# An audio tower on one core: the code is masked where it lies in PSUM, a ring of three banks, and small matmuls on halves of the array

## The chip, the cores and the metric

The kernel runs on one core of a Trainium2 chip. A core has TensorE (matmuls, results go to PSUM banks), ScalarE, VectorE, GpSimd (which works in SBUF) and DMA queues started here by SyncE. The metric is the device time of one execution in microseconds (us), the median of several runs.

## The reference

The input is `x` (16 items of 750 rows by 64). Each item goes through two layers. Layer 0: a recurrent token mixer with a strided 15-tap convolution (750 rows become S = 375), a retention with rotary embedding, and a product-key memory. Layer 1: a gradient step on a small two-layer model, then an expert layer for each item. Nearly all of the time is the product-key memory. Cut to what matters, it is, for each of 8 heads:

```python
sim = einsum('pbnhd,pkhd->pbnhk', q, pk_keys)          # p = 2 halves, 64 keys each
scores, idx = top_k(sim, 16)
score = scores[0][..., :, None] + scores[1][..., None, :]  # 256 candidates
final_scores, pk_idx = top_k(score, 16)
weights = softmax(final_scores)                         # on 16 of 4096 slots
# the 16 slots' keys and values are summed with these weights, then attended to
```

A row's 16 final slots, out of 64 x 64 = 4096, get softmax weights. Keys and values of the table (4096 x 8 heads, 64 + 64 columns) are summed with these weights for each of the 375 rows. An attention over the 375 sums per head and an output projection follow.

## The kernel before

One item has 375 rows, which stand in the free dimension (or as 3 tiles of 125 rows). VectorE finds for each row the 16 best keys of either half (`pick_rows`, the search) and turns them into three *factors* per head: `ranksT` (for each key of one half its rank, and how far the other half may reach), `first_of` (the exponential of the first half's score, fp32) and `second_of` (that of the second half, in bf16 pieces, two factors). The 16 x 4096 choice is never gathered. Instead the kernel rebuilds the dense weights of 128 table slots at a time. That is a *step*. There are 32 steps a head, 256 an item (`STEPS`), 4096 in all, and each goes through three engines in a software pipeline (`dense_slot`):

1. TensorE, the code (L527): `hot` x `ranksT` gives a value that is at most 0 where the slot was chosen and positive where it was not, in the bank `coded`.
2. ScalarE, the mask (L910): relu of the code, written as bf16 to `past` in SBUF.
3. TensorE, the spread (L506): the second half's values, spread over the 128 slots, and behind it in the same bank L508, which subtracts 1024 x `past` by a matmul with the diagonal `far`.
4. ScalarE (L905): relu of that bank to `dense_w` in SBUF. What was masked becomes 0. `taken` counts this.
5. GpSimd (L451, `weigh`): `dense_w` times `first_of`, in place.
6. TensorE (L520): table x `dense_w`, fp32, two instructions, summed over the head's 32 steps in `accu`.

A *slot* j of the pipeline holds on TensorE, in this order: the spread of step j-2, a factor if one is due, the sum of step j-6, the code of step j. On ScalarE it holds: `dense_w` of step j-2, the copy of a factor if one is due, the mask of step j. Each engine takes its own instructions strictly in that written order, and semaphores join them. `bank_free` makes TensorE wait until the bank that it is about to write was read. Before, the spreads and factors took turns in two banks (item n waits for item n-2), and `coded` was a third bank of its own, so that the code of step j waits for the mask of step j-1.

Factors of head 0 are made ahead of slot 0. Those of the other heads come in every second slot, in slots 0 to 6 and 30 to 76, one each, 28 in all: `ranksT` and the two `second_of` in bf16, `first_of` in fp32.

The rest of an item's work is written between slots, by constants (`FILL_PREPARE`, `STEPS_A`, ...). `prepare` is the token mixer, convolution and retention of item b+2 (33 slots in between). `gradient` is layer 1 of item b (30 slots). Then come 108 slots beside the search, with `similarities` (L608) in three places. `attention` holds the other 91 slots: per head the scores (L638), the query projection of head h+2 (L631), 5 slots, `mix` of head h-1 (L644), the transposes (L684), and 5 slots more. ScalarE's exponentials (L977) stand between its two groups of slots. After the last item a short tail runs the expert layer.

In this tower a matmul of 64 rows runs on a row half of the array, one of 64 output columns on a column half.

## Time and profile before

| | |
|---|---|
| median of 3 runs | 6943.39 us (6937.87 to 6958.16) |
| the profiled execution's own time | 6937.05 us |
| its span | 6935.2 us |
| TensorE busy | 6277.6 us, 91% of the span |
| ScalarE busy | 4668.2 us, 67% |
| GpSimd busy | 4397.3 us, 63% |
| VectorE busy | 4120.9 us, 59% |
| chain that ended last | TensorE 71%, GpSimd 12%, ScalarE 10%, VectorE 6% |
| mean granted TensorE clock | 0.983 of full speed |

A matmul's time in the trace runs from its start to the landing of its last column, so matmuls that follow each other overlap in the records. What a matmul costs TensorE is the distance from its start to the next one's start. In the same way ScalarE's instructions overlap: what one costs is the distance between starts. An item takes about 400 us in the steady part (the stretch from 3000 to 3400 us is one, and rows below are from it).

### The profile page before, as it was taken

How to read it: one execution, taken by the hardware profiler on the slowest of the kernel's cores; microseconds unless marked ns; L12 is line 12 of the kernel's file. 1: busy time of each engine (PE TensorE's matmuls, PEld its weight loads, DVE VectorE, ACT ScalarE, POOL GpSimd, SP SyncE). 2: the span in 40 equal slices, each digit the busy share in tenths (PEclk: the TensorE clock that was granted, in tenths of full speed). 3: DMA queues.
4: the chain of work that ended last, by engine and by line, in shares of the span. 5: the costliest groups of instructions: out<-in, count | busy, mean ns of one | idle time of the engine just before them, and what ended most of it. 6: DMA issues, size and time to landing. Idle time of an engine off the chain costs nothing.

```text
span 6935.2 us, 87978 instructions
## 1 busy us (share of the span) xinstructions
PE 6277.6 (91%) x28800; PEld 3567.8 (51%) x28800; DVE 4120.9 (59%) x13328; ACT 4668.2 (67%) x10873; POOL 4397.3 (63%) x4108
## 2 busy tenths in 40 slices
PE   2799999999999999999999999999999999999977
PEld 1455555555555555555555555555555555555533
DVE  7564847647484764748575574757557475752147
ACT  0676777767677776767676777767777776767733
POOL 0575857758585775858576585857668585766600
PEclk9999999999999999999999999999999999999978
DMA  1111111111111111111111111111111111111100
GB/s 33 43 49 38 46 42 43 48 37 48 38 49 39 45 47 37 49 36 49 39 46 45 37 49 36 52 36 46 46 36 49 38 51 37 46 47 43 44 19 15
DMA packets 93493, 290.94 MB, mean 42 GB/s; under 512 B 17879, under 2 KB 26546, under 8 KB 92780
## 3 DMA queue, kind: packets, MB, share of 16 engines
q1 hardware_dynamic: 92748, 285.25, 12.4%
q8 instruction: 229, 3.75, 0.2%
q14 instruction: 228, 1.87, 0.1%
q10 hardware_dynamic: 288, 0.07, 0.0%
HBM read 280.68 MB, written 4.61 MB: 41 GB/s over the span
## 4 chain that ended last, share of the span: by engine, by line
PE 71%; POOL 12%; ACT 10%; DVE 6%; issue 2%; DMA 0%; SPq 0%; DVEq 0%; ACTq 0%
PE accu L520 29%; POOL dense_w L451 12%; PE dense L527 8%; PE dense L506 7%; PE dense L508 7%; PE sims L638 3%; PE work L644 2%; ACT past L910 2%; PE work L631 1%; PE work L566 1%; PE sims L608 1%; PE work L684 1%; PE dense L492 1%; ACT dense_w L905 1%; PE work L618 1%
## 5 line engine op out<-in xcount | busy, mean ns | idle before, releaser
L451 POOL TENSOR_TENSOR dense_w<-dense_w,store 128x375 f32<-128x375 f32 x4096 | 4394.9, 1088 | 2208.8 <-ACT dense_w L905 2126.5
L520 PE MATMUL accu<-dense_w,store 128*128 128x375 f32 x8192 | 3284.0, 484 | 151.7 <-POOL dense_w L451 101.0
L910 ACT ACTIVATE past<-dense 128x375 bf16<-128x375 f32 x4096 | 1982.5, 484 | 1118.3 <-PE dense L527 1090.0
L905 ACT ACTIVATE dense_w<-dense 128x375 f32<-128x375 f32 x4096 | 1966.8, 480 | 177.2 <-PE dense L508 172.2
L520 PEld LDWEIGHTS accu<-dense_w,store 128*128 128x128 f32 x8192 | 1408.5, 190 | 473.7 <-POOL dense_w L451 125.7
L527 PE MATMUL dense<-store,hot 128*128 128x375 bf16 x4096 | 1326.2, 324 | 116.8 <-ACT past L910 115.7
L506 PE MATMUL dense<-store,spread 96*128 96x375 bf16 x4096 | 1335.9, 326 | 25.5 <-ACT dense_w L905 25.4
L508 PE MATMUL dense<-past,far 128*128 128x375 bf16 x4096 | 1329.5, 325 | 0.0
L527 PEld LDWEIGHTS dense<-store,hot 128*128 128x128 bf16 x4096 | 394.8, 96 | 955.3 <-ACT past L910 813.5
L506 PEld LDWEIGHTS dense<-store,spread 96*128 96x128 bf16 x4096 | 399.8, 98 | 714.1 <-issue 323.1
L508 PEld LDWEIGHTS dense<-past,far 128*128 128x128 bf16 x4096 | 405.7, 99 | 228.4 <-issue 13.4
L1291 DVE TENSOR_TENSOR picks<-codes,keys 125x4096 uint16<-125x4096 uint16 x192 | 500.2, 2605 | 6.0 <-ACTq L897 0.6
L1340 DVE TENSOR_TENSOR shared<-sims,mask 125x750 f32<-125x750 f32 x64 | 60.1, 940 | 722.5 <-PE sims L638 722.5
L1299 DVE TENSOR_REDUCE store<-picks 125x256 bf16<-125x2048 uint16 x192 | 438.9, 2286 | 6.6
L1296 DVE TENSOR_TENSOR picks<-picks 125x2048 uint16<-125x2048 uint16 x192 | 343.6, 1789 | 6.6
L1340 DVE TENSOR_TENSOR prob_odd<-sims,mask 125x750 f32<-125x750 f32 x64 | 60.0, 938 | 306.2 <-PE sims L638 306.2
L644 PE MATMUL work<-shared 125*64 125x375 f32 (+2 forms) x768 | 191.8, 385 | 10.3 <-ACT shared L1009 10.3
L638 PE MATMUL sims<-kvT,two_q 64*125 64x125 f32 (+2 forms) x768 | 200.2, 395 | 0.2 <-ACT kvT L915 0.2
L1361 DVE TENSOR_TENSOR h<-h_now,work 125x192 f32<-125x192 f32 x16 | 5.7, 354 | 288.5 <-PE work L693 288.5
L972 ACT ACTIVATE two_q<-work 64x375 f32<-64x375 f32 x128 | 61.0, 477 | 168.5 <-PE work L631 168.5
L608 PE MATMUL sims<-simw,n2T 64*125 64x512 f32 x192 | 100.3, 644 | 77.9 <-DVE i L1239 68.3
L1228 DVE FIND_INDEX8 i<-s,front 125x8 uint32<-125x64 f32 x768 | 166.7, 217 | 0.0
(255 smaller groups left out, 6499.5 us busy)
## 6 DMA issues: line engine op xcount, KB each, us to landing
store<-in SPq DMA_DIRECT2D x513, 512.0 KB, 3.3
x_in<-in SPq DMA_DIRECT2D x16, 187.5 KB, 2.4
store<-in SPq DMA_DIRECT2D x1, 2048.0 KB, 9.1
queries_kept<-n3T SPq DMA_DIRECT2D x16, 93.8 KB, 3.6
h_saved<-h SPq DMA_DIRECT2D x16, 93.8 KB
store<-queries_kept SPq DMA_DIRECT2D x16, 93.8 KB, 2.5
store<-h_saved SPq DMA_DIRECT2D x16, 93.8 KB
out<-store SPq DMA_DIRECT2D x16, 93.8 KB
```

The lines of the kernel that those rows point to most:

```text
L451: nc.gpsimd.tensor_tensor(dense_w[:, i % RING, :], dense_w[:, i % RING, :], first_of[:, i // CHUNKS, :], ALU.mult).then_inc(s["weighed"], 1)
L506: mm(to[:, 0:S], spread[0:3 * I1S, c % (CHUNKS // GROUPS), :], second_of[0:3 * I1S, c // (CHUNKS // GROUPS), h, :], start=True, stop=False)
L508: mm(to[:, 0:S], far[:], past[:, i % 2, :], start=False, stop=True).then_inc(s["spread"], 1)
L520: last = mm(accu[:, 0, 0:S], table[:, n % PIECE_RING, i % PIECE, :], dense_w[:, i % RING, :], start=(c == 0), stop=(c == CHUNKS - 1))
L527: mm(coded, hot[:, j % CHUNKS, :], ranksT[:, j // CHUNKS, :], start=True, stop=True).then_inc(s["coded"], 1)
L638: last = mm(dst, qT[:, h % 2, tile(i)], kvT[0:D, h, 0:(i + 1) * P], start=True, stop=True)
L644: last = mm(work[D:128, 0, j * P:S], vo[:, j, h * D:(h + 1) * D], pT[:, min(j, 1), (0, 0, 2 * P)[j]:(S, 2 * P, S)[j]], start=(h == 0 and j ...
L905: fn(dense_w[:, i % RING, :], dense[:, n % 2, 0:S], ACT.Relu).then_inc(s["taken"], 1)
L910: fn(past[:, j % 2, :], coded, ACT.Relu).then_inc(s["past"], 1)
L1291: v.tensor_tensor(hit, codes[:, h:h + 2].unsqueeze(3).broadcast_to([P, 2, 2, SUB, K]), keys[:].unsqueeze(1).unsqueeze(1).broadcast_to([P, ...
L1296: v.tensor_tensor(hit[:, :, :, :, 0:K // 2], hit[:, :, :, :, 0:K // 2], hit[:, :, :, :, K // 2:], ALU.min).then_inc(s["pick_step"], 1)
L1299: v.tensor_reduce(ranks[:, t, h:h + 2, :].rearrange("p h (a i) -> p h a i", a=2), hit[:, :, :, :, 0:K // 2], AX_X, ALU.min).then_inc(s["pi ...
```

## The change

It has these parts:

- `far`, `past` and the matmul L508 are gone. ScalarE's mask now reads the code in its PSUM bank and writes relu(1024 x code) back to the same bank in fp32. The `spread` table has its sign turned, so that the spread matmul, now with `start=False`, adds minus the seconds to what lies in the bank. The second relu has `scale=-1.0`.
- A step therefore holds one bank from its code (slot j) to its `dense_w` (slot j+2). Steps and factors take turns in three banks (`BANKS`). `bank_free` waits for item n-3. The spread waits for the mask of its own step. Factors have semaphores of their own.
- `similarities`: `n2T` lies twice, in rows 0 to 63 and 64 to 127, and `simw` is split, so that the two matmuls of a tile stand on different row halves. ScalarE makes one more copy per item.
- `queries`: `wq_s` has 128 rows, the lower 64 zero, and the moving operand has 128 rows. It is written behind the first group of slots, right ahead of `mix`, and ScalarE's `scale_q` behind the exponentials. Scores: `qT` has 128 rows with the lower 64 zero, and `kvT` is used whole.

```diff
-            if 0 <= j - SPREAD_LAG < STEPS:
-                items.append(("spread", j - SPREAD_LAG))
             if self.factor_at(j) is not None:
                 items.append(("factor", self.factor_at(j)))
+            if j < STEPS:
+                items.append(("step", j))
...
-            def bank_free(n):
-                if n >= 2:
-                    pe.wait_ge(s["taken"], n - 1)
-                return dense[:, n % 2]
+            def bank_free(b, n):
+                if n >= BANKS:
+                    kind, what = ORDER.items[n - BANKS]
+                    if kind == "step":
+                        pe.wait_ge(s["taken"], what + 1)
+                    else:
+                        pe.wait_ge(s["factor_kept"], (b * H + what[0]) * FACTORS + what[1] + 1)
+                return dense[:, n % BANKS]
...
-                    to = bank_free(ORDER.spread[i])
-                    if j > STEPS:
-                        pe.wait_ge(s["past"], i + 1)
-                    mm(to[:, 0:S], spread[0:3 * I1S, c % (CHUNKS // GROUPS), :], second_of[0:3 * I1S, c // (CHUNKS // GROUPS), h, :],
-                       start=True, stop=False)
-                    mm(to[:, 0:S], far[:], past[:, i % 2, :], start=False, stop=True).then_inc(s["spread"], 1)
+                    pe.wait_ge(s["past"], i + 1)
+                    mm(dense[:, ORDER.step[i] % BANKS, 0:S], spread[0:3 * I1S, c % (CHUNKS // GROUPS), :],
+                       second_of[0:3 * I1S, c // (CHUNKS // GROUPS), h, :],
+                       start=False, stop=True, skip_group_check=True).then_inc(s["spread"], 1)
...
                 if j < STEPS:
-                    if j >= 1:
-                        pe.wait_ge(s["past"], j)
-                    mm(coded, hot[:, j % CHUNKS, :], ranksT[:, j // CHUNKS, :], start=True, stop=True).then_inc(s["coded"], 1)
+                    if j % CHUNKS == 0:
+                        pe.wait_ge(s["factor_kept"], (b * H + j // CHUNKS + 1) * FACTORS)
+                    to = bank_free(b, ORDER.step[j])
+                    mm(to[:, 0:S], hot[:, j % CHUNKS, :], ranksT[:, j // CHUNKS, :], start=True, stop=True,
+                       skip_group_check=True).then_inc(s["coded"], 1)
...
                 for c in range(2):
-                    last = mm(sims[0:P, c, :], n2T[:, tile(t)], simw[:, c * 512:(c + 1) * 512], start=True, stop=True)
+                    half = slice(c * D, (c + 1) * D)
+                    last = mm(sims[0:P, c, :], n2T[half, tile(t)], simw[half], start=True, stop=True)
...
-                    mm(work[0:D, 0, 0:S], wq_s[:, h], n2T_now, start=True, stop=True).then_inc(s["q_mm"], 1)
+                    mm(work[0:D, 0, 0:S], wq_s[:, h], halves[:, S:2 * S], start=True, stop=True).then_inc(s["q_mm"], 1)
...
-                        last = mm(dst, qT[:, h % 2, tile(i)], kvT[0:D, h, 0:(i + 1) * P], start=True, stop=True)
+                        last = mm(dst, qT[:, h % 2, tile(i)], kvT[:, h, 0:(i + 1) * P], start=True, stop=True)
...
-                    if h + 2 < H:
-                        queries(h + 2)
                     if h < NEXT_FROM:
                         fill(b, STEPS_A[h])
                     elif following:
-                        if h == NEXT_FROM:
-                            pe.wait_ge(s["taken"], FACTORS)
                         fill(b + 1, STEPS_A[h])
+                    if h + 2 < H:
+                        queries(h + 2)
...
-                    fn(dense_w[:, i % RING, :], dense[:, n % 2, 0:S], ACT.Relu).then_inc(s["taken"], 1)
+                    fn(dense_w[:, i % RING, :], dense[:, ORDER.step[i] % BANKS, 0:S], ACT.Relu, scale=-1.0).then_inc(s["taken"], 1)
...
-                    fn(past[:, j % 2, :], coded, ACT.Relu).then_inc(s["past"], 1)
+                    here = dense[:, ORDER.step[j] % BANKS, 0:S]
+                    fn(here, here, ACT.Relu, scale=FAR).then_inc(s["past"], 1)
...
-                nc.scalar.copy(n2T[:], work[0:D, 1, 0:S]).then_inc(s["nT_done"], 1)
+                nc.scalar.copy(n2T[0:D], work[0:D, 1, 0:S])
+                nc.scalar.copy(n2T[D:128], work[0:D, 1, 0:S]).then_inc(s["nT_done"], 1)
...
-    spread = np.where(row < 3 * I1S, row % I1S == 2 * chunk + key // SUB, False).astype(f).reshape(128, CHUNKS // GROUPS * 128)
+    spread = -np.where(row < 3 * I1S, row % I1S == 2 * chunk + key // SUB, False).astype(f).reshape(128, CHUNKS // GROUPS * 128)
```

On TensorE, in `prepare` of a later item, two slots of the dense steps with a factor (L494) in the first stand in a row so before. Rows are in program order, with what each waits for; L506 is the spread, L508 the subtraction, L520 the sum, L527 the code.

```order
L506 MATMUL dense<-store,spread 128x375 [waits taken]
L508 MATMUL dense<-past,far 128x375
L494 MATMUL dense<-ident_b,store 96x125 [waits taken]
L494 MATMUL dense<-ident_b,store 96x125 x2
L520 MATMUL accu<-dense_w,store 128x375 [waits weighed]
L527 MATMUL dense<-store,hot 128x375 [waits past]
L506 MATMUL dense<-store,spread 128x375 [waits taken]
L508 MATMUL dense<-past,far 128x375
L520 MATMUL accu<-dense_w,store 128x375 [waits weighed]
L527 MATMUL dense<-store,hot 128x375 [waits past]
```

The same two slots of the changed kernel, where the code is L528 and the factor L496:

```order
L506 MATMUL dense<-store,spread 128x375 [waits past]
L496 MATMUL dense<-ident_b,store 96x125 [waits factor_kept]
L496 MATMUL dense<-ident_b,store 96x125 x2
L520 MATMUL accu<-dense_w,store 128x375 [waits weighed]
L528 MATMUL dense<-store,hot 128x375 [waits taken]
L506 MATMUL dense<-store,spread 128x375 [waits past]
L520 MATMUL accu<-dense_w,store 128x375 [waits weighed]
L528 MATMUL dense<-store,hot 128x375 [waits taken]
```

L508 is gone. The wait on `past` has moved from the code to the spread, and the one on `taken` from the spread to the code, which now stands last in a slot.

On TensorE at the start of a head of the attention, before (L638 the scores, L631 the query projection of head h+2, then the first slot):

```order
L638 MATMUL sims<-kvT,two_q 125x125 [waits s_masked,q_done]
L638 MATMUL sims<-kvT,two_q 125x250
L638 MATMUL sims<-kvT,two_q 125x375
L631 MATMUL work<-halves,wo_s 64x375
L506 MATMUL dense<-store,spread 128x375 [waits taken]
L508 MATMUL dense<-past,far 128x375
L520 MATMUL accu<-dense_w,store 128x375 [waits weighed]
```

In the changed kernel the same projection (L634) stands behind the last of the head's first five slots and ahead of `mix` (L647), with the transposes (L685) behind:

```order
L506 MATMUL dense<-store,spread 128x375 [waits past]
L520 MATMUL accu<-dense_w,store 128x375 [waits weighed]
L528 MATMUL dense<-store,hot 128x375 [waits taken]
L634 MATMUL work<-halves,wq_s 64x375
L647 MATMUL work<-shared 64x375 [waits pT_done]
L647 MATMUL work<-shared 64x250
L647 MATMUL work<-shared 64x125
L685 MATMUL work<-ident,prob_odd 125x125 [waits s_norm]
```

The projection has moved from between the scores and the slots to the place beside `mix`, whose output goes to the other column half (partitions 64 to 127 of the same bank). This pairing exists for heads h = 1 to 5 of an item.

## Rows read from the trace of the kernel before

**Rows 1.** The page: busy time of the engines, and TensorE's granted clock.
```profile
PE 6277.6 (91%) x28800; PEld 3567.8 (51%) x28800; DVE 4120.9 (59%) x13328; ACT 4668.2 (67%) x10873; POOL 4397.3 (63%) x4108
...
PEclk9999999999999999999999999999999999999978
```

**Rows 2.** The page's groups: busy us, mean ns of one | idle before, releaser.
```profile
L451 POOL TENSOR_TENSOR dense_w<-dense_w,store 128x375 f32<-128x375 f32 x4096 | 4394.9, 1088 | 2208.8 <-ACT dense_w L905 2126.5
...
L910 ACT ACTIVATE past<-dense 128x375 bf16<-128x375 f32 x4096 | 1982.5, 484 | 1118.3 <-PE dense L527 1090.0
...
L508 PE MATMUL dense<-past,far 128*128 128x375 bf16 x4096 | 1329.5, 325 | 0.0
```

**Rows 3.** Timeline of one plain step: start us, us, engine, line, operation, count.
```profile
3246.55 0.32 PE L527 MATMUL dense<-store,hot 128*128 128x375 bf16 x1
...
3246.71 0.32 PE L506 MATMUL dense<-store,spread 96*128 96x375 bf16 x1
...
3246.87 0.32 PE L508 MATMUL dense<-past,far 128*128 128x375 bf16 x1
...
3246.91 0.48 ACT L910 ACTIVATE past<-dense 128x375 bf16<-128x375 f32 x1 [0.26 <-PE dense L527]
...
3247.03 0.79 PE L520 MATMUL accu<-dense_w,store 128*128 128x375 f32 x2
...
3247.29 0.48 ACT L905 ACTIVATE dense_w<-dense 128x375 f32<-128x375 f32 x1
...
3247.66 0.32 PE L527 MATMUL dense<-store,hot 128*128 128x375 bf16 x1
```

**Rows 4.** Timeline of a step with a bf16 factor in it.
```profile
3121.77 0.32 PE L506 MATMUL dense<-store,spread 96*128 96x375 bf16 x1
...
3122.09 0.33 PE L494 MATMUL dense<-ident_b,store 125*96 125x125 bf16 x3
...
3122.26 0.85 PE L520 MATMUL accu<-dense_w,store 128*128 128x375 f32 x2
...
3123.11 0.32 PE L506 MATMUL dense<-store,spread 96*128 96x375 bf16 x1
```

**Rows 5.** Waits: how long in total, how often, and the longest.
```profile
PE dense L527 <- ACT past L910: 115.7, 134, 2.3
```

**Rows 6.** Windows: stretch, busy us (count) of PE, PEld, DVE, ACT, POOL; clock, DMA, GB/s.
```profile
3160.00:3290.00 130.00, 120.09 (x507) 64.84 (x506) 109.32 (x279) 92.96 (x212) 118.17 (x100) 0.99 0.16 53
```

**Rows 7.** Timeline, GpSimd and VectorE, in the same stretch.
```profile
3163.16 15.75 POOL L451 TENSOR_TENSOR dense_w<-dense_w,store 128x375 f32<-128x375 f32 x12 [2.58 <-ACT dense_w L905]
...
3186.62 30.32 POOL L451 TENSOR_TENSOR dense_w<-dense_w,store 128x375 f32<-128x375 f32 x24
...
3199.28 3.04 DVE L1291 TENSOR_TENSOR picks<-codes,keys 125x4096 uint16<-125x4096 uint16 x1
...
3257.29 38.32 POOL L451 TENSOR_TENSOR dense_w<-dense_w,store 128x375 f32<-128x375 f32 x30 [1.93 <-ACT dense_w L905]
```

**Rows 8.** Timeline of TensorE at the start of a head.
```profile
3308.23 0.32 PE L527 MATMUL dense<-store,hot 128*128 128x375 bf16 x1
...
3308.48 1.53 PE L638 MATMUL sims<-kvT,two_q 64*125 64x125 f32 x6
...
3309.95 0.84 PE L631 MATMUL work<-halves,wo_s 64*64 64x375 f32 x2
...
3310.72 0.33 PE L506 MATMUL dense<-store,spread 96*128 96x375 bf16 x1
```

**Rows 9.** Timeline of TensorE: matmuls on row halves and on column halves.
```profile
3053.76 0.90 PE L556 MATMUL work<-front,wtok_s 64*128 64x375 f32 x4
...
3159.68 1.98 PE L608 MATMUL sims<-simw,n2T 64*125 64x512 f32 x4
...
3109.86 0.47 PE L710 MATMUL work<-n3T,mv_s 64*64 64x375 f32 x1
...
3109.87 0.53 PE L712 MATMUL work<-n3T,mlrb 64*64 64x375 f32 x1
```

More of the change, by code:

```diff
@@ L47 @@
 FAR = 1024.0
+BANKS = 3
 FILL_PREPARE = (2, 2, 2, 3, 6, 4, 4, 4, 6)
@@ L71, in __init__ @@
     def __init__(self):
-        self.spread, self.factor = {}, {}
+        self.step, self.factor = {}, {}
         items = [("factor", (0, k)) for k in range(FACTORS)]
         for j in range(SLOTS):
-            if 0 <= j - SPREAD_LAG < STEPS:
-                items.append(("spread", j - SPREAD_LAG))
             if self.factor_at(j) is not None:
                 items.append(("factor", self.factor_at(j)))
+            if j < STEPS:
+                items.append(("step", j))
         for n, (kind, what) in enumerate(items):
-            (self.spread if kind == "spread" else self.factor)[what] = n
-        self.items = len(items)
-        assert self.items % 2 == 0
+            (self.step if kind == "step" else self.factor)[what] = n
+        self.items = items
+        assert len(items) % BANKS == 0
     @staticmethod
@@ L194, in tower @@
         h1 = sb("h1", [P, NT, D])
-        n2T = sb("n2T", [D, S])
+        n2T = sb("n2T", [128, S])
         s16 = sb("s16", [P, 2 * H, K])
@@ L225, in tower @@
         hot = sb("hot", [128, CHUNKS, 128], BF16)
-        far = sb("far", [128, 128], BF16)
         edge = sb("edge", [128, 1])
@@ L292, in tower @@
             h_mm h_act y_mm lg_mm lg_d y_bias lg_exp wy wy_sum pe_waits act_waits dve_waits sp_waits
-            pool_waits pick_step upd_step choice_step coded past spread taken begun factors_out weighed
+            pool_waits pick_step upd_step choice_step coded past spread taken factored factor_kept begun factors_out weighed
             acc_done piece_out hot_in hot_done""".split()
@@ L448, in weigh @@
             def weigh(i):
-                pool.wait_ge(s["taken"], ORDER.spread[i] + 1)
+                pool.wait_ge(s["taken"], i + 1)
                 nc.gpsimd.tensor_tensor(dense_w[:, i % RING, :], dense_w[:, i % RING, :], first_of[:, i // CHUNKS, :],
@@ L495, in factor @@
                                   start=True, stop=True)
-                last.then_inc(s["spread"], 1)
+                last.then_inc(s["factored"], 1)
             def dense_slot(b, j):
@@ L740, in count_anew @@
             def count_anew():
-                nc.tensor.sem_inc(s["taken"], -ORDER.items)
+                nc.tensor.sem_inc(s["taken"], -STEPS)
                 nc.tensor.sem_inc(s["past"], -STEPS)
@@ L827, in _ @@
             begin(0)
-            pe.wait_ge(s["taken"], FACTORS)
             fill(0, EARLY)
@@ L875, in keep @@
                 nc.scalar.copy(h1_now[:], h1[:])
-                nc.scalar.copy(n2T_now, n2T[:]).then_inc(s["kept"], 1)
+                nc.scalar.copy(n2T_now, n2T[0:D]).then_inc(s["kept"], 1)
             slot = [0]
@@ L886, in keep_factor @@
                 n = ORDER.factor[h, k]
-                act.wait_ge(s["spread"], n + 1)
-                src = dense[:, n % 2, 0:S]
+                act.wait_ge(s["factored"], (b * H + h) * FACTORS + k + 1)
+                src = dense[:, n % BANKS, 0:S]
                 if k == 0:
@@ L894, in keep_factor @@
                     last = nc.scalar.copy(second_of[0:3 * I1S, k - 2, h, :], src[0:3 * I1S])
-                last.then_inc(s["taken"], 1)
+                last.then_inc(s["factor_kept"], 1)
                 if (h, k) == (H - 1, FACTORS - 1):
@@ L1046, in count_anew @@
             def count_anew():
-                nc.scalar.sem_inc(s["spread"], -ORDER.items)
+                nc.scalar.sem_inc(s["spread"], -STEPS)
                 nc.scalar.sem_inc(s["coded"], -STEPS)
```

27 lines of the change are left out of this document (13 added, 14 removed).

## The prediction

> **What bounds the kernel now.** I read the page's busy times first, then its groups, then the timeline of single steps, then the waits. TensorE is busy 6277.6 of 6935.2 us at nearly full clock [rows 1]. The steps are all of this kernel: 4096 of them, each with a relu on ScalarE before and after the spread, and a product on GpSimd of 1.088 us in the mean, about the length of a step [rows 2]. The timeline shows what one step costs TensorE where nothing else is in between: from one code matmul (L527) to the next, 3246.55 to 3247.66, 1.11 us [rows 3]. It is filled: code 0.16, spread 0.16, the subtraction L508 0.16, the two fp32 passes of the sum 0.63. In this stretch TensorE waits for nobody. So what is taken off TensorE counts, until ScalarE, the ring of banks or GpSimd sets the step.
>
> **ScalarE in a plain step.** L910 starts at 3246.91, 0.36 after its code matmul started, and L905 at 3247.29, so an instruction costs ScalarE 0.38 though it is recorded with 0.48 [rows 3]. Two cost 0.76 of a step of 1.11. A matmul that waits for ScalarE I take to start 0.05 to 0.06 after the end of the recorded time.
>
> **The far matmul: -659 us.** Each step loses one start-to-start distance of L508, 3246.87 to 3247.03, 0.16 in the rows and 0.161 in the trace's nanoseconds [rows 3], 4096 times [rows 2]. A plain step would take 0.95. ScalarE fits with 0.76. The new chain fits too. Count from the start of a slot: the code starts at 0.79, the mask at 0.79 + 0.36 = 1.15, it is visible at 1.15 + 0.48 + 0.06 = 1.69, and the spread that waits for it stands two slots on, at 1.90. The code of the next slot needs a bank whose `dense_w` was read long before. So plain steps (206 of the 262 slots of an item) keep the gain.
>
> **The ring beside factors: +128.** In slots 0 to 7 and 30 to 77 there are three ring items in two slots: step, step, factor. With three banks item n-3 is then always the step two before. So the code of step j waits for `dense_w` of step j-2, which ScalarE can only make after the spread in the same slot. From the slot's start: the mask of step j-1 starts at 0.20, L905 behind it at 0.58, visible at 0.58 + 0.48 + 0.06 = 1.11 or so, and only then the code, 0.16. The slot takes 1.27. Before, a plain one took 1.11, and one with a bf16 factor 1.34 (3121.77 to 3123.11) [rows 4]. One with the fp32 factor (six passes of 125 columns, a third of 0.315 each, 0.63 or a bit more) takes some 1.79, and after the change 1.62, since there TensorE's own work is longer than the wait. Per item: 28 x 1.27 + 21 x 1.27 + 7 x 1.62 = 73.6 us after, 28 x 1.11 + 21 x 1.34 + 7 x 1.79 = 71.7 before. These 56 slots gain nothing, though the first term counted 56 x 0.161 = 9.0 for them: 10.9 us an item to give back. Where other matmuls stand ahead of a slot, the mask of step j-1 is out of the way and the wait shrinks by 0.22; some twelve blocks of slots begin in this region. I take 8 us an item, 128 in all. Ends: 0 (if waits that are there anyway cover it) and 175 (16 x 10.9).
>
> **GpSimd in the search: +75.** In the 130 us of the search stretch GpSimd is busy 118.2 for 100 steps [rows 6]. It runs without a gap through six pieces of 89 steps, for instance 24 steps in 30.32 us and 30 in 38.32 [rows 7]: 1.27 a step, far over the 0.95 that TensorE would need. The reason is VectorE: beside a search instruction of 3.04 us [rows 7] GpSimd's product takes as long, against 1.088 in the mean [rows 2]. That part belongs to the items' searches and not to the steps, and stays. The records of neighbours overlap by 0.04, so GpSimd needs 118.2 - 4 = 114 us there; TensorE without L508 needs 130 - 16.1 = 114 with its present waits in it. Two engines that both need 114 and have four steps of room between them take more: I give back 5 us an item in 15 items, 75. Ends: 30, and 215 (89 x 0.161 x 15, if none of the unbroken pieces gets shorter).
>
> **Scalar interruptions: +27.** In the attention three exponentials and a copy stand between two slots on ScalarE, and TensorE's code waits for them: 115.7 us in 134 waits [rows 5]. After such an interruption the second slot can start once `dense_w` and mask are through, E + 0.92 where E is its end; before, the code did at E + 0.92, and the slot behind at E + 1.08. That is 0.16 sooner, but TensorE arrives 2 x 0.161 sooner too. 0.16 more each, 134 x 0.16 = 21. The second copy of `n2T` stands on the path to `similarities`: one ScalarE distance of 0.38 [rows 3], 16 times, 6.
>
> **Similarities on row halves: -41.** Four passes take 1.98 us [rows 9], each 512 columns of fp32, 0.43. In the same trace four passes on alternate row halves (L556, 375 columns, four times 0.315) are through in 0.90, so halves overlap [rows 9]. Two passes fewer, 0.85, 48 times. Ends: 0 (VectorE, whose search step before the second one is through 6 us ahead, comes late) and 41.
>
> **Queries and scores: -81.** From L631 to the next slot it takes 0.77, and the scores' last pass before it is longer than 0.315 by 0.09 [rows 8]. The step from code to scores takes 0.25 (3308.23 to 3308.48) where to a spread it takes 0.16 [rows 3, 8]: changing between a half and the whole array costs 0.09. Beside `mix` the projection uses the other column half. That column halves overlap the trace shows in L710 and L712, whose passes start 0.01 apart [rows 9]. Five heads an item save 0.77 + 0.09, all eight save 0.09 at the scores: 5.0 an item, 81. Ends: 10 (only the 0.09s of the scores) and 81.
>
> The Trainium skill, "TensorEngine Tiling (Array Packing)", Key Properties, says that changing the tiling mode drains the array and that tiles of one mode run in parallel. The trace agrees on both: 0.09 us for a change, and a start 0.01 later.
>
> **The sum.** -659 + 128 + 75 + 27 - 41 - 81 = -551. Against the profiled execution's 6937.05 (span 6935.2) that is 6386. The median of the runs is 6.3 above it, so I say 6392.
>
> **One cost that no row shows** is that of a ScalarE instruction with its output in PSUM, in the bank that it reads. The nearest rows are those with the same input and output in SBUF, 0.484 bf16 [rows 2] and 0.48 fp32 [rows 3], at a distance of 0.38. From below: it may be shorter, which only makes the slack of 0.21 in a plain step larger. From above: reading and writing take turns in the bank, and the distance doubles to 0.76. I take 0.38, the rows that differ by the target alone.
>
> The Trainium skill, "ScalarE: Activation LUTs", in "Step-by-step: what each stage is for", says that ScalarE reaches PSUM faster than SBUF. No run so far shows it. By that rule the doubling is unlikely; my sum doesn't use it.
>
> **Rivals.**
> - *The clamps are stronger.* GpSimd keeps its unbroken pieces (215 instead of 75) and the ring costs its full 175 instead of 128: 6392 + 140 + 47 = 6579. For it: GpSimd's pieces have no gap [rows 7]. Against: it is 4 us below the stretch's length in sum.
> - *The clamps hardly bite.* Ring 0, GpSimd 30, interruptions as now: 6392 - 128 - 45 - 27 = 6192. For it: there are waits in these stretches that would hide some of it. Against: the wait of the code for `dense_w` of step j-2 follows from the order of instructions.
> - *The halves don't overlap here.* Only the 0.09 changes are saved: 6392 + 41 + 71 = 6504. Against it: two places of this trace.
> - *Slower: ScalarE's in-place mask takes turns.* At a distance of 0.76 a plain step needs 0.76 + 0.38 = 1.14 of ScalarE, no gain over 1.11. Beside factors L905 starts at 0.96 instead of 0.58, and the slot takes 1.65, 0.38 more in 49 slots of 16 items, 298. Plain slots lose 0.03 x 206 x 16 = 99. The halves give 122. 6943 + 298 + 99 + 48 - 122, the 48 being longer interruptions, is 7266. It decides from a distance of about 0.6.
> - *The matmul is not gone from the path* (the time stays within 0.3%): only if ScalarE's distance lies near 0.55 to 0.6.
>
> **How the numbers follow.** Forecast 0.55, with its own range 6310 to 6480; stronger clamps 0.17; weak clamps 0.13; no overlap 0.08; slower 0.05; no change 0.02. A difference within 0.3% is about what a measurement of this kernel can't tell from none. Faster is the sum of the first four, 0.93. The range of 8 in 10 reaches from 6250, short of the weak clamps' end, to 6580, which takes in the strong ones and no overlap.
>
> **What would show it.** Plain slots with code to code at 0.95 (right) or 1.1 (ScalarE or the ring took it back). Slots 30 to 77 in `prepare` and `gradient` with 1.27 and a wait of the code for the second relu, which now should be the largest new wait of TensorE. In the search stretch GpSimd busy nearly throughout, at a length of some 118 us instead of 130. ScalarE's in-place mask at 0.48 or less. The first passes of `similarities` and of queries and `mix` starting within 0.01 of each other. The prediction is wrong if the in-place mask is long, if the clock granted falls well below 0.98 through many short waits, or if VectorE's search becomes what the search stretch waits for.

## The result and the profile after

The changed kernel takes 6541.34 us (median of three, 6530.81 to 6542.57) against 6943.39: 0.9412 of the time, interval 0.9385 to 0.944, 402 us less. The forecast was 6392. So the sign is right and the time lies in the range, but 149 us above the forecast, outside the likeliest case's own range of 6310 to 6480, and nearer to the rival "the clamps are stronger" (6579).

The page of the changed kernel, busy times, granted clock and groups, answers to [rows 1, 2]:

```profile
PE 5693.9 (87%) x24704; PEld 3145.4 (48%) x24704; DVE 4115.3 (63%) x13330; ACT 4642.1 (71%) x10889; POOL 4415.3 (68%) x4108
...
L449 POOL TENSOR_TENSOR dense_w<-dense_w,store 128x375 f32<-128x375 f32 x4096 | 4412.9, 1098 | 1786.2 <-ACT dense_w L904 1746.1
...
L910 ACT ACTIVATE dense<-dense 128x375 f32<-128x375 f32 x4096 | 1917.5, 468 | 909.7 <-PE dense L528 682.0
```

TensorE's share of the span fell from 91 to 87%: it lost 584 us of work, and the span fell by 406. The in-place mask takes 468 ns where the one to SBUF took 484. This is the first row of such a relu with its target in PSUM. The Trainium skill, "ScalarE: Activation LUTs", "Step-by-step: what each stage is for", says that ScalarE reaches PSUM faster than SBUF. The recorded times agree, by 16 ns against the old mask (bf16) and by 12 against the second relu (L904, fp32 to SBUF, 480 ns).

One plain step after, the timeline of TensorE and ScalarE, answers to [rows 3]:

```profile
3126.54 0.32 PE L528 MATMUL dense<-store,hot 128*128 128x375 bf16 x1
...
3126.70 0.32 PE L506 MATMUL dense<-store,spread 96*128 96x375 bf16 x1
...
3126.90 0.47 ACT L910 ACTIVATE dense<-dense 128x375 f32<-128x375 f32 x1
...
3127.28 0.48 ACT L904 ACTIVATE dense_w<-dense 128x375 f32<-128x375 f32 x1
3127.49 0.32 PE L528 MATMUL dense<-store,hot 128*128 128x375 bf16 x1
```

Code to code is 0.95 instead of 1.11, and the distance of the two relus, which is what one costs, is still 0.38. Beside factors the same timeline reads otherwise (answers to [rows 4]):

```profile
2918.95 0.32 PE L528 MATMUL dense<-store,hot 128*128 128x375 bf16 x1
...
2919.32 0.47 ACT L910 ACTIVATE dense<-dense 128x375 f32<-128x375 f32 x1
2919.70 0.48 ACT L904 ACTIVATE dense_w<-dense 128x375 f32<-128x375 f32 x1
...
2920.23 0.33 PE L528 MATMUL dense<-store,hot 128*128 128x375 bf16 x1 [0.15 <-ACT dense_w L904]
...
2920.56 0.83 PE L494 MATMUL dense<-ident,store 125*128 125x125 f32 x6
...
2921.86 0.32 PE L528 MATMUL dense<-store,hot 128*128 128x375 bf16 x1
```

The slot from 2918.95 takes 1.28 although TensorE has only 0.95 of work in it: `dense_w` of step j-2 ends at 2920.18, and the code starts 0.05 later. The next, with an fp32 factor, takes 1.63. In the waits this is TensorE's largest, and beside it the wait for GpSimd's product has grown from 101.0 us before:

```profile
PE dense L528 <- ACT dense_w L904: 253.3, 494, 2.3
...
PE accu L520 <- POOL dense_w L449: 162.2, 196, 1.8
```

The small matmuls, the timeline of TensorE, answers to [rows 8, 9]: similarities in 1.13 instead of 1.98, and query passes (L634) starting 0.01 from those of `mix` (L647):

```profile
2983.34 1.13 PE L611 MATMUL sims<-simw,n2T 64*125 64x512 f32 x4
...
3147.63 0.53 PE L634 MATMUL work<-halves,wq_s 128*64 128x375 f32 x1
3147.64 0.53 PE L647 MATMUL work<-shared 125*64 125x375 f32 x1
```

Windows over the parts of one item, cut at its code matmuls. Before, slots 0 to 7, 30 to 81, 82 to 189 (search) and 190 to 255 (attention); columns as in [rows 6]:

```profile
3014.27:3026.26 11.99, 10.01 (x59) 5.93 (x57) 2.97 (x8) 9.96 (x27) 5.43 (x6) 1.00 0.01 1
3067.61:3156.08 88.47, 82.39 (x431) 48.28 (x430) 46.22 (x175) 64.40 (x148) 52.84 (x52) 1.00 0.13 42
3156.08:3296.90 140.82, 130.91 (x560) 71.34 (x558) 113.17 (x318) 100.73 (x230) 126.61 (x109) 0.99 0.15 52
3296.90:3416.15 119.25, 114.56 (x523) 65.51 (x522) 67.79 (x275) 82.52 (x210) 67.75 (x68) 1.00 0.14 45
```

The same parts of the same item after, and in the last line slots 0 to 7 of the item behind it:

```profile
2839.06:2851.91 12.85, 9.21 (x52) 5.11 (x49) 3.04 (x8) 10.03 (x27) 5.47 (x6) 1.00 0.01 1
2890.35:2980.23 89.88, 79.38 (x380) 41.57 (x380) 43.16 (x172) 64.71 (x149) 53.08 (x53) 0.98 0.13 41
2980.23:3112.27 132.04, 114.67 (x452) 60.30 (x451) 113.11 (x322) 100.42 (x230) 128.52 (x109) 0.97 0.17 55
3112.27:3214.61 102.34, 98.05 (x457) 58.34 (x455) 70.08 (x274) 81.03 (x210) 67.22 (x68) 1.00 0.16 53
...
3214.61:3232.29 17.68, 14.53 (x51) 8.03 (x49) 3.04 (x8) 10.29 (x27) 5.70 (x7) 0.61 0.00 1
```

Three things are to be seen. GpSimd is busy 128.52 of the 132.04 us of the search, where it had 14 us to spare before. The attention got 17 us shorter, the first two parts slightly longer. And slots 0 to 7 take 12.85 us at a granted clock of 1.00 (2.4 GHz), but 17.68 in the next item at 0.61, most of it at the lower level (1.2 GHz, 0.5). From the fifth item on such items alternate in the changed kernel.

The parts of an item in all kernels, means over ten items (the fourth to the thirteenth) in us. The columns go by the numbers of the code matmuls. The last one counts the steps of the whole program whose code matmul ran at half clock: it is recorded with over 400 ns, where it has some 330 otherwise. The kernels named r1 to r11 are the experiments below.

| kernel | 0-7 | 8-29 | 30-81 | 82-189 | 190-255 | item | half clock |
|---|---|---|---|---|---|---|---|
| before | 12.35 | 41.35 | 89.68 | 140.79 | 119.56 | 403.7 | 34 |
| after | 15.64 | 38.44 | 90.67 | 132.30 | 102.35 | 379.4 | 128 |
| r1_banks | 11.60 | 38.44 | 84.23 | 132.18 | 102.36 | 368.8 | 73 |
| r2_room | 14.83 | 39.79 | 90.87 | 127.76 | 104.95 | 378.2 | 109 |
| r3_far_only | 14.04 | 38.44 | 92.00 | 133.40 | 108.41 | 386.3 | 88 |
| r4_fill_ring | 15.15 | 38.53 | 90.70 | 132.23 | 102.36 | 379.0 | 93 |
| r5_fill_search | 15.48 | 38.44 | 90.76 | 139.15 | 102.37 | 386.2 | 120 |
| r7_short_after | 15.59 | 38.44 | 90.17 | 120.39 | 102.35 | 367.0 | 73 |
| r8_short_before | 12.21 | 41.35 | 89.05 | 132.27 | 119.23 | 394.1 | 33 |
| r9_small_only | 12.00 | 41.35 | 88.58 | 139.19 | 113.56 | 394.7 | 33 |
| r10_light_search | 14.16 | 38.44 | 88.94 | 124.58 | 102.36 | 368.5 | 50 |
| r11_both_again | 11.27 | 38.45 | 85.9 | 128.03 | 104.95 | 368.6 | 60 |

Against the forecast, per item: 0 to 7 and 30 to 81 together -2.1 forecast (60 slots at -0.161, 8 given back for the ring, and -0.5 for one group of the similarities with the second copy, which stand there), +4.3 measured (102 us of the miss in 16 items); the search -14.1 and -8.5 (90); 8 to 29 -3.5 and -2.9 (10); the attention -14.3 and -17.2 (-46). That makes 156. The miss is 149: the first and the last item gained more than steady ones, and the forecast charged GpSimd in 15 items, not 16.

### The profile page after: what moved, and what is told of

It reads as the page before. It is cut to its first block, busy times and chain, and to the rows that moved or that the text cites. A ratio compares the mean times of both kernels' runs of the same rounds, so it can differ in the third digit from the quotient of the medians.

```text
span 6529.0 us, 79900 instructions
## 1 busy us (share of the span) xinstructions
PE 5693.9 (87%) x24704; PEld 3145.4 (48%) x24704; DVE 4115.3 (63%) x13330; ACT 4642.1 (71%) x10889; POOL 4415.3 (68%) x4108
## 4 chain that ended last, share of the span: by engine, by line
PE 60%; POOL 16%; ACT 15%; DVE 6%; issue 2%; DMA 0%; SPq 0%; DVEq 0%; ACTq 0%
PE accu L520 27%; POOL dense_w L449 16%; PE dense L528 9%; PE dense L506 7%; ACT dense L910 4%; ACT dense_w L904 3%; PE sims L641 2%; PE work L647 2%; PE work L568 1%; PE work L685 1%; PE dense L494 1%; PE work L634 1%; PE work L621 1%; PE dense L816 1%; ACT prob_odd L978 1%
## 5 line engine op out<-in xcount | busy, mean ns | idle before, releaser
L520 PE MATMUL accu<-dense_w,store 128*128 128x375 f32 x8192 | 3369.9, 494 | 227.9 <-POOL dense_w L449 162.2
L910 ACT ACTIVATE dense<-dense 128x375 f32<-128x375 f32 x4096 | 1917.5, 468 | 909.7 <-PE dense L528 682.0
L904 ACT ACTIVATE dense_w<-dense 128x375 f32<-128x375 f32 x4096 | 1965.1, 480 | 217.9 <-PE dense L506 216.2
L520 PEld LDWEIGHTS accu<-dense_w,store 128*128 128x128 f32 x8192 | 1449.1, 196 | 568.1 <-issue 203.0
L528 PE MATMUL dense<-store,hot 128*128 128x375 bf16 x4096 | 1347.6, 330 | 254.9 <-ACT dense_w L904 253.3
L506 PE MATMUL dense<-store,spread 96*128 96x375 bf16 x4096 | 1355.7, 331 | 13.9 <-ACT dense L910 11.2
L528 PEld LDWEIGHTS dense<-store,hot 128*128 128x128 bf16 x4096 | 397.8, 97 | 1129.8 <-ACT dense_w L904 710.6
L506 PEld LDWEIGHTS dense<-store,spread 96*128 96x128 bf16 x4096 | 403.9, 99 | 806.8 <-ACT dense L910 533.7
L1299 DVE TENSOR_TENSOR picks<-picks 125x2048 uint16<-125x2048 uint16 x192 | 343.5, 1789 | 6.6
L647 PE MATMUL work<-shared 125*64 125x375 f32 (+2 forms) x768 | 201.5, 400 | 10.4 <-ACT shared L1010 10.4
L641 PE MATMUL sims<-kvT,qT 128*125 128x125 f32 (+2 forms) x768 | 184.7, 376 | 0.2 <-ACT kvT L915 0.2
L1231 DVE FIND_INDEX8 i<-s,front 125x8 uint32<-125x64 f32 x768 | 165.7, 216 | 0.0
L1232 DVE MATCH_REPLACE8 front<-s,front 125x64 f32<-125x64 f32 x768 | 158.2, 206 | 0.0
L1247 DVE TENSOR_TENSOR cand<-s 125x16 f32<-125x16 f32 (+5 forms) x384 | 155.9, 475 | 1.1
L1221 DVE MAX8 s<-front 125x8 f32<-125x64 f32 x768 | 101.9, 211 | 84.5 <-ACT front L956 83.9
L1242 DVE FIND_INDEX8 i<-s,front 125x8 uint32<-125x64 f32 x768 | 150.2, 218 | 0.0
```

The costliest lines, as they stand in the source:

```text
L506: mm(dense[:, ORDER.step[i] % BANKS, 0:S], spread[0:3 * I1S, c % (CHUNKS // GROUPS), :], second_of[0:3 * I1S, c // (CHUNKS // GROUPS), h, ...
L520: last = mm(accu[:, 0, 0:S], table[:, n % PIECE_RING, i % PIECE, :], dense_w[:, i % RING, :], start=(c == 0), stop=(c == CHUNKS - 1))
L528: mm(to[:, 0:S], hot[:, j % CHUNKS, :], ranksT[:, j // CHUNKS, :], start=True, stop=True, skip_group_check=True).then_inc(s["coded"], 1)
L641: last = mm(dst, qT[:, h % 2, tile(i)], kvT[:, h, 0:(i + 1) * P], start=True, stop=True)
L647: last = mm(work[D:128, 0, j * P:S], vo[:, j, h * D:(h + 1) * D], pT[:, min(j, 1), (0, 0, 2 * P)[j]:(S, 2 * P, S)[j]], start=(h == 0 and j ...
L904: fn(dense_w[:, i % RING, :], dense[:, ORDER.step[i] % BANKS, 0:S], ACT.Relu, scale=-1.0).then_inc(s["taken"], 1)
```

## Experiments

The theory for the first part: the banks, taken in turn, make the code wait. **Banks by earliest release** chooses for each item the bank whose last user is read first, so that a factor's bank is used again at once:

```diff
-        assert len(items) % BANKS == 0
+        for n, (kind, what) in enumerate(items):
+            j = what if kind == "step" else self.slot_of(what)
+            at = min(range(BANKS), key=lambda k: free_at[k])
+            self.bank.append(at)
+            self.waits_for.append(user[at])
+            free_at[at], user[at] = 3 * (j + SPREAD_LAG) if kind == "step" else 3 * j + 1, n
...
-                return dense[:, n % BANKS]
+                return dense[:, ORDER.bank[n]]
```

> One change against the changed kernel: the three banks are not taken in turn; each step or factor takes the bank whose last user is read earliest, so that in the slots beside factors the odd steps find a bank free at once (a factor's bank is free within its slot) and only the even ones wait for the second relu of the step two before. Ring theory (the missing time lies mainly in the 56 slots beside factors, where a code waits for that relu): odd slots go from 1.27 to 0.95-1.0 us, the stretches of slots 30 to 81 lose about 7 to 9 us an item together, the whole 100 to 140 us, to about 6400-6440. Rival (the waits there only stand in for waits on ScalarE's and VectorE's chains of the token mixer and the gradient step, which come late anyway): odd slots get shorter but the stretches don't, 0 to 40 us. Clock theory (short waits pull TensorE's granted clock down, and that is what costs): fewer steps at half clock in slots 30 to 81 than the 30 now.

Measured: 6376.32 us (6372.56 to 6383.96), ratio 0.9182 [0.9166, 0.9197], 165 less than the changed kernel and more than the 100 to 140 expected. By the table all of it is in slots 0 to 7 and 30 to 81, 10.5 an item; fewer steps at half clock are a part of that (in slots 0 to 81, 23 instead of 62). The windows of slots 0 to 7 and 30 to 81 of the same item:

```profile
2777.71:2789.31 11.60, 9.33 (x51) 5.25 (x49) 3.04 (x8) 9.83 (x27) 5.15 (x6) 1.00 0.01 1
2827.75:2911.08 83.33, 75.27 (x380) 41.15 (x379) 44.67 (x173) 64.63 (x149) 52.78 (x53) 1.00 0.13 44
```

The timeline of its TensorE beside factors (L540 the code, L518 the spread, L508 the bf16 factor, L506 the fp32 one):

```profile
2855.33 0.32 PE L540 MATMUL dense<-store,hot 128*128 128x375 bf16 x1
...
2857.05 0.32 PE L540 MATMUL dense<-store,hot 128*128 128x375 bf16 x1
...
2858.01 0.32 PE L540 MATMUL dense<-store,hot 128*128 128x375 bf16 x1
2858.17 0.32 PE L518 MATMUL dense<-store,spread 96*128 96x375 bf16 x1
2858.50 0.37 PE L508 MATMUL dense<-ident_b,store 125*96 125x125 bf16 x3
...
2859.40 0.32 PE L540 MATMUL dense<-store,hot 128*128 128x375 bf16 x1
```

The slot without a factor (2857.05 to 2858.01) takes 0.96, not 1.28: the ring theory holds. A slot with a factor takes 1.39 and 1.72 here. Its medians in the trace, 1.27 and 1.72, are hardly below the 1.34 and 1.78 of before. The bf16 factor starts 0.33 behind its spread, as it did before with the subtraction in between (3121.77 to 3122.09, [rows 4]). What it waits for now stands at TensorE's weight loads (PEld) in the same slot:

```profile
2858.50 0.22 PEld L508 LDWEIGHTS dense<-ident_b,store 125*96 125x96 bf16 x3 [0.40 <-ACT dense_w L916]
...
2859.28 0.10 PEld L540 LDWEIGHTS dense<-store,hot 128*128 128x128 bf16 x1 [0.32 <-ACT dense_w L916]
```

The bf16 factor waits for a second relu (L916) that frees its bank, and the code behind it for the next one. In the changed kernel the factors' weight loads show no such wait. Here they show 256, by the list of waits:

```profile
PEld dense L508 <- ACT dense_w L916: 54.3, 160, 0.8
PEld dense L506 <- ACT dense_w L916: 45.7, 96, 1.9
```

So this version takes the ring's wait from the slots without a factor, as expected, and not from those with one. It is no kernel without a ring.

**The three parts apart.** First the small matmuls undone (halves, projection beside `mix`, scores over 128 rows), with the ring kept:

```diff
-                    half = slice(c * D, (c + 1) * D)
-                    last = mm(sims[0:P, c, :], n2T[half, tile(t)], simw[half], start=True, stop=True)
+                    last = mm(sims[0:P, c, :], n2T[:, tile(t)], simw[:, c * 512:(c + 1) * 512], start=True, stop=True)
```

> Against the changed kernel: the matmuls of the search are again on one row half, queries and scores again with 64 rows and the projection at its old place; what is left of the change is the in-place mask and the ring of three banks. Forecast's sizes: the small matmuls were worth 41 + 81 - 6 = 116 us, so this one takes 6541 + 116 = about 6657, with the attention stretch 5 us an item longer and every similarities group 0.85 longer. Rival (they hide under waits, above all in the search stretch, which GpSimd sets): 60 to 90 us, about 6600 to 6630, all of it in the attention stretch.

Measured: 6642.91 us (6637.3 to 6653.89), 0.9565 [0.9549, 0.9581]. The small matmuls are worth 102 on top of the ring, between the 116 of the forecast's sizes and the 60 to 90 of the rival. Alone, in the kernel before:

> The kernel before with the other half of the change alone: similarities on row halves, queries beside mix and zero-padded, scores over 128 rows; the far matmul, `past` and the two-bank ring stay. The changed kernel and the one without these parts differ by about 100 us. If the parts are independent, this one takes 6941 - 100 = about 6840. If the head's chain (ScalarE's query scaling now behind the exponentials) or the search stretch swallows a part: 6860 or more.

Measured: 6791.23 us (6789.04 to 6801.19), 0.9785 [0.977, 0.98], so 152 us below the kernel before by its median (149 against the runs beside it), where about 100 was expected. The parts alone make about 300 and 149, together 402: 47 are lost. By the table the small matmuls bring 6.0 us an item in the attention either way. Where they are lost is slots 0 to 7 (-0.35 alone, +1.6 on the ring, which is half clock) and the search (-1.6 alone, -1.1 on the ring). With a gain of 0.2 more in slots 30 to 81 that is 35 of the 47; the rest lies outside these ten items.

**Is there cover in the ring's slots?** A useless bf16 matmul ahead of the wait for the product, in the slots 0 to 7 and 30 to 77 that hold a sum other than a head's first. These are slot 7 and 46 of slots 30 to 77, 752 in the program:

```diff
+                    if c >= 1 and (j < 8 or 30 <= j < 78):
+                        mm(accu[:, 0, 0:S], nought[:], hot[:].rearrange("p c k -> p (c k)")[:, 0:S], start=False, stop=False,
+                           skip_group_check=True)
```

> Against the changed kernel: in the slots beside factors (0 to 7, 30 to 77) TensorE runs one more bf16 matmul of 375 columns with zero weights, which adds 0 to the running sum, ahead of the sum's two passes. Ring theory: TensorE waits 0.16 to 0.32 in these slots anyway, so the extra 0.16 costs nothing in slots with 1.27, and 0.16 only in the 7 slots with the fp32 factor and at a block's start: 0 to 30 us slower. Clock theory: fewer idle moments keep the granted clock up, steps at half clock in slots 30 to 81 go from 30 to about 10 and the time falls by 10 to 40 us. Rival (no ring wait, TensorE is simply busy there): 56 x 0.16 x 16 = 143 us slower.

Measured: 6535.94 us (6530.34 to 6538.33), 0.9412 [0.9396, 0.9427]. It costs nothing in sum, where the rival asked for 143 us; the rival is out. But two things cancel in this sum. Where no step is at half clock, slots 30 to 81 take 89.8 instead of 88.7, so 1.1 us of the 46 x 0.161 = 7.4 is felt, about what the expectation charges to the slots with an fp32 factor. And 8 steps instead of 30 are at half clock there, as the clock theory expected. TensorE has the idle time in most of these slots, not in each.

**What bounds the search?** The same matmul in slots 82 to 189:

> Against the changed kernel: the useless bf16 matmul (zero weights, 375 columns, added to the running sum) now stands in the 108 slots beside the search (82 to 189) and not in those beside factors. It puts back there the TensorE time that the removed subtraction gave. GpSimd theory (GpSimd is busy 127.3 of the stretch's 132.3 us, TensorE waits for it): 108 x 0.161 = 17 us an item of TensorE time cost only what TensorE lacks in waits, 2 to 6 us an item, 30 to 100 us in all. Rival (TensorE still sets the stretch): 16 x 17 = 278 us slower. Clock theory: more activity, so fewer of the 66 steps at half clock in that stretch; if those matter, the time even falls.

Measured: 6655.57 us (6644.46 to 6664.71), 0.9585 [0.9569, 0.9601]: 114 more than the changed kernel, a little over the 30 to 100 expected, of the 270 that its 1680 matmuls would cost on TensorE's path; 6.9 of 17 us an item. Its search window:

```profile
3036.88:3175.69 138.81, 127.41 (x556) 69.46 (x555) 113.44 (x322) 100.44 (x230) 127.88 (x109) 1.00 0.17 51
```

TensorE and GpSimd are now both busy for some 127 us, and the stretch takes 11 more than either. Two engines with equal loads cost more here than the larger load. That it is the little room between them was not tested in this kernel.

**GpSimd shortened**, its product on 250 of 375 columns, in the changed kernel and in the one before. Both leave out part of the computation and show only the time:

```diff
-nc.gpsimd.tensor_tensor(dense_w[:, i % RING, :], dense_w[:, i % RING, :], first_of[:, i // CHUNKS, :],
+nc.gpsimd.tensor_tensor(dense_w[:, i % RING, 0:250], dense_w[:, i % RING, 0:250], first_of[:, i // CHUNKS, 0:250],
```

> Against the changed kernel: GpSimd multiplies only 250 of the 375 columns of each step, the other 125 go unweighted (this leaves out part of the computation, and shows only the time). GpSimd theory: its product falls to about two thirds, the search stretch falls from 132.3 us an item to what TensorE needs, 132.3 - 16 of waits = about 116, so 230 to 260 us less in all, about 6290. VectorE theory (VectorE is busy 128.0 of that stretch as well, and the search is what it waits for): the stretch stays above 125, less than 110 us gained.

> The kernel before with the same cut, 250 of 375 columns on GpSimd (part of the computation left out). With r7_short_after it tells what the removed subtraction is worth in the search stretch once GpSimd doesn't set it. GpSimd theory: here the stretch falls from 140.8 to about 131-133 us an item (its waits for GpSimd, some 8 us, go), 110 to 150 us in all, about 6800-6830; the two short kernels differ in that stretch by 16 to 19 us an item, where before and after differ by 8.5. VectorE theory: both short kernels stay at 125 us or more and differ by less than 10.

Measured: 6346.39 us (6330.05 to 6369.36), 0.9147 [0.9121, 0.9173], and 6793.93 (6792.69 to 6797.86), 0.9791 [0.9775, 0.9808]. The changed kernel loses 195 us, less than the 230 to 260 of the GpSimd theory and more than the 110 of the VectorE theory. The search falls to 120.4 in the one and 132.3 in the other. So GpSimd holds up both kernels there, the one before by 8.5 us an item, the changed one by 11.9. Between the two short kernels lie 11.9 us, less than the 16 to 19 that the subtraction and the similarities would give with GpSimd out of the way: neither theory is met. The window after:

```profile
2899.78:3020.31 120.53, 111.80 (x451) 60.03 (x450) 104.27 (x314) 100.42 (x230) 100.27 (x109) 0.99 0.19 60
```

TensorE is busy 93% of it, VectorE 87%. Which of them holds the last microseconds I can't say. VectorE is busy 104.27 us in it and was 113.11 in the changed kernel, although only GpSimd's work was cut. So the 11.9 are what GpSimd's shorter product brings by itself and through VectorE.

**Why GpSimd takes so long there.** VectorE's folding (L1299) on 1 of 64 keys, which again leaves out part of the computation:

```diff
-                    v.tensor_tensor(hit[:, :, :, :, 0:K // 2], hit[:, :, :, :, 0:K // 2], hit[:, :, :, :, K // 2:],
+                    v.tensor_tensor(hit[:, :, :, 0:1, 0:K // 2], hit[:, :, :, 0:1, 0:K // 2], hit[:, :, :, 0:1, K // 2:],
```

> The changed kernel with VectorE's folding step of the search (1789 ns, 192 times, 12 an item, of which 8 in the search stretch) cut to one of 64 keys, GpSimd as it is (part of the computation left out). In the search stretch VectorE is busy 128 and GpSimd 127 of 132 us, and they hold each other up. Theory of the shared time: the 8 x 1.8 = 14 us leave VectorE and, with them, the part for which GpSimd's products were held up: GpSimd's busy time in the stretch falls by 6 us or more and the stretch by 5 to 10 us an item, 80 to 160 us in all. GpSimd alone (its products would take that long anyway): its busy time stays at 125 or more and the stretch above 129.

Measured: 6377.27 us (6364.7 to 6384.81), 0.9193 [0.9179, 0.9207], 164 less. By the table 7.7 us an item of it are in the search, some 124 us; most of the rest is in slots 0 to 7 and 30 to 81, where fewer steps are at half clock. The group of GpSimd's product in the search window, in the changed kernel:

```profile
L449 POOL TENSOR_TENSOR dense_w<-dense_w,store 128x375 f32<-128x375 f32 x109 | 129.1, 1222 | 3.4 <-ACT dense_w L904 2.8
```

and in this one:

```profile
L449 POOL TENSOR_TENSOR dense_w<-dense_w,store 128x375 f32<-128x375 f32 x109 | 121.1, 1146 | 3.6 <-ACT dense_w L904 3.1
```

VectorE's folding in the same two windows, first the changed kernel:

```profile
L1299 DVE TENSOR_TENSOR picks<-picks 125x2048 uint16<-125x2048 uint16 x8 | 14.5, 1818 | 0.3
```

then this one:

```profile
L1299 DVE TENSOR_TENSOR picks<-picks 125x32 uint16<-125x32 uint16 x8 | 6.1, 767 | 0.3
```

GpSimd does the same 109 products and needs 8.0 us less for them, because VectorE does 8.4 us less; the stretch gets 7.7 shorter. GpSimd idles only 3.4 and 3.6 us in it. That VectorE's work lengthens GpSimd's is shown, and that GpSimd's time sets the length of this stretch too.

**More room between the engines**: sum two steps later, seven buffers of `dense_w`. An item then has 264 slots, and the two new ones stand at the end of the search.

```diff
-SPREAD_LAG, SUM_LAG, RING = 2, 6, 6
+SPREAD_LAG, SUM_LAG, RING = 2, 8, 7
-FILL_SECOND = (18, 14, 30)
+FILL_SECOND = (18, 14, 32)
```

> One change against the changed kernel: the sum stands 8 slots behind the code instead of 6 (ring of 7 dense_w tiles instead of 6, two more slots at the end of the search stretch), so that TensorE and GpSimd have six steps of room between them instead of four. GpSimd-room theory (the search stretch takes 132.3 us where GpSimd is busy 127.3, because a long product empties the room): 3 to 5 us an item less in the search stretch, 45 to 80 us in all. Rival (GpSimd and VectorE are simply full there, their shared work is the limit): less than 25 us either way.

Measured: 6521.62 us (6518.81 to 6525.49), 0.9394 [0.9379, 0.941], 20 less, which is the rival's size (less than 25) and not the 45 to 80 of the room theory. The attention begins at slot 192 here (and in r11_both_again), so the 4.5 less and 2.6 more of the table's columns belong together. From slot 82 to the attention's first slot it takes 131.0 instead of 132.3, and the attention 101.7 instead of 102.3. Room is not what is lacking.

**Both**, the banks and the room, first in three rounds:

> Bank choice by earliest release (r1_banks, 6376 us) and two more steps of room between TensorE and GpSimd (r2_room, 20 us under the changed kernel) together. If the two are independent: 6376 - 20 = 6356 us. If the room only filled the waits that the ring made: 6376.

Measured: 6363.82 us (6362.06 to 6366.65), 0.9171 [0.9156, 0.9186], between the two expectations. Then in five, beside the banks alone on the same chip:

> Bank choice and two more steps of room, again, five rounds beside r12_banks_again on the same chip. Before it was 6364 against 6376 us on different calls: 8 to 16 us below r12 if the room is worth something by itself, within 4 us of it if not. Against the kernel before a ratio of 0.917.

> Bank choice alone, again, five rounds: 6376 us, 0.918 of the kernel before.

Measured: 6366.02 us (6364.13 to 6370.2), 0.9174 [0.9162, 0.9187], and 6373.98 (6373.7 to 6379.7), 0.9189 [0.9176, 0.9201]. The lowest and highest of the two don't meet: the room is worth 8 us, and the banks by earliest release carry the rest. Both versions beat the kernel before and the changed one.

## Why the prediction was right in sign and 149 us too low

**The far matmul: right.** Plain steps take 0.95, as forecast, and 8 to 29, where no factor stands, gave 2.9 an item of the 3.5 counted.

**ScalarE's in-place mask: right.** 468 ns at a distance of 0.38; the slower rival needed 0.6.

**The ring beside factors: the wait was right, the deduction from it failed.** The slots take 1.28, 1.28 and 1.63 in the median, forecast 1.27, 1.27 and 1.62. The code's wait for the second relu is TensorE's largest. From these lengths the prediction had 10.9 us an item to give back to its first term, and it charged only 8, because at some twelve starts of blocks the wait would shrink by 0.22. That did not come. Read where no step is at half clock, slots 0 to 7 and 30 to 81 take 12.0 and 88.5 before, 12.85 and 88.7 after (the 88.7 in one item of this trace, and in eleven of r10_light_search). They grew by 1.1 an item, and by 1.5 without the 0.4 that the similarities saved there (88.1 in r9_small_only). Slots 78 to 81, which have no factor, gained 0.6 of their own. So the slots of the ring grew by 2.1, and with the 9.0 that the first term had counted for them the ring cost 11.1 an item, 178 in all: just above the upper end of 175, not 128. Of the starts of blocks some gained (slots 38, 42, 46 and 54 are 0.15 shorter than before, a slot with a bf16 factor in a row only 0.05), others lost as much (slots 31 and 32 together are 0.30 longer). 3.1 an item is 50 us. r1_banks takes 11.6 and 83.3 in these parts and so gets 6.6 of the 11.1 back, 106 us. What a kernel without any wait for a bank would get back no run shows.

**The granted clock: named as what could go wrong, but at no price.** It went from 0.983 to 0.964. An item whose slots 0 to 7 run at full clock takes 12.8 there, one with four steps at half clock 17.7, and every second item does. The means above those of full-clock items are 2.8 (0 to 7), 2.0 (30 to 81) and 0.5 (search, 131.8 without) after, and 0.35 and 1.2 before: 3.8 an item, about 60 us. The stretch where it fell is the one in which TensorE waits most: 9.21 busy of 12.85 us, against 10.01 of 11.99 before. In r1_banks, with 9.33 of 11.60, it stays at full clock there from the third item on. That the waits cause it is not shown. r4_fill_ring put work into slot 7 alone of slots 0 to 7, where they took 15.15 instead of 15.64 in the mean, so it doesn't settle this; and why it comes in every second item is open.

**GpSimd in the search: the right engine, a size too small.** I charged 75 and it was about 157 (75 plus the 82 of the search's miss that isn't clock), within the ends of 30 and 215. The step that failed is "two engines that both need 114". The 118.17 of [rows 6] is the time in which GpSimd is busy at all, so overlapping records count in it once; the lengths of its hundred records there add up to 120.97. Taking another 4 off for the overlap made GpSimd TensorE's equal, which it was not. Over the whole stretch it is busy 126.61 of 140.82 us, and TensorE needs some 121.7 there by the forecast's own terms (140.8 less 17.4 and 1.7). In the changed kernel GpSimd is busy 128.52 for the same 109 products, and the stretch takes 132.04. So 4.9 lie between the two needs, 1.9 are GpSimd's own growth and 3.5 its idle time, 10.3 an item, where 5 was charged. The second half of the step, that the shared time with VectorE stays, was right: r10_light_search took a part of it away and 7.7 us went.

**Scalar interruptions, queries and scores: too dear and too cheap.** The attention gave 17.2 an item instead of 14.3. By r3_far_only the ring change alone gave 11.15, which is 66 slots at 0.161 and 0.5: the interruptions, charged 21 in all, cost nothing. By r9_small_only the halves and the moved projection gave 6.0, not 5.0. Together -46.

**The likeliest case.** 50 + 60 + 82 - 46 + 10 is 156, and the ends of the program take 7 off. The time of the "stronger clamps" rival is near, and its reasons hold in part: its 47 for the ring came, of its 140 for GpSimd 82 came. The clock, which had no price in it, added 60, and the attention took 46 off. That its time is met to 38 us, and that the time lies in the range in spite of the clock, is partly luck.

## What to carry to other kernels

A wait that the order of instructions forces is charged in full, unless a row shows what covers it: here a deduction for the starts of blocks, with no row behind it, was 46 us too much. The busy time of a window counts overlapping instructions once, so nothing is to be taken off it again. Where another engine's need is within a few per cent of what the bound engine will need, take the larger as the new length and add for the clash. A ring of banks whose items live for different times should be handed out by earliest release and not in turn: here this gave 165 us for a few lines of planning, 106 of them in slots at full clock.

## What was not expected of the hardware

A product of the same shape on GpSimd takes 1.222 us in the mean in the search and 1.146 when VectorE's eight foldings an item take 0.767 us instead of 1.818: 8.0 us of GpSimd's time for 8.4 of VectorE's. And the same slots of the same kernel were granted 1.00 in one item and 0.61 in the next, in turn, at 4.8 us each time, which is more than the 0.9 that the waits themselves had added there. The cause of the turn is not shown.
